# The seam between experts and attention: maxima turned one tile sooner, first scores around k's projection, q and y copied by VectorE

## The chip, the cores and the metric

The kernel runs on one core of one Trainium2 chip. The metric is device time in microseconds of one execution, as the median of several runs. Lower is better.

## The reference, cut to what matters

```python
# x: (8, 512, 128): 8 batches of 512 tokens, 16 heads of 8, 8 experts of width 176, 2 chosen, a shared expert of 352
xn = layernorm(x)
qkv = xn @ w_in.T + b_in                       # q, k, v to 16 heads of 8
scores = (q / sqrt(8)) @ k.T + causal_bias
attn = softmax(scores) @ v                     # then @ w_out.T + b_out, NaN to 0
p = softmax(xn @ gate_w.T)                     # router: 2 largest, normalised, times 2.5 -> combine
y = sum_e combine[:, e] * (silu(xn @ w_gate[e]) * (xn @ w_up[e])) @ w_down[e]
y += (silu(xn @ sw_gate) * (xn @ sw_up)) @ sw_down
out = x + attention + y
```

Everything is float32.

## The kernel before, in words

The five engines each have a program written out by hand, in order, with semaphores between them; nothing reorders it. The work goes batch by batch. For a batch `b` there are two stages, and the program loops over them with the next batch's preparation mixed in:

- **Experts and maxima** (`experts_and_maxima`, the first batch has its own `first_experts_and_maxima`). The 1408 routed and 352 shared hidden columns make `NT` = 14 tiles. For tile `k` TensorE runs `gate_up` (six matmuls, L537 to L539, each product split into high and low float32r parts), ScalarE takes `silu` (L871), POOL weighs it with the router's numbers (L1016, routed tiles), VectorE multiplies by the up half (`hidden`, L1229), ScalarE rounds to the high part (`high_hidden`, L878), POOL takes the low part (`low_hidden`, L1024); VectorE does these two itself for the last tiles (L1237, L1244). Two tiles later TensorE runs `down` (L553 to L555), which adds into `bank_y`. In between, TensorE computes the attention scores a first time, and VectorE takes each row's maximum (L1253). When all are there, VectorE splits the maxima into three bf16 parts (L1274, L1277), TensorE turns them (`transpose_maxima`, L617), ScalarE copies them out (`max_rows`, L900), and a transfer on SP's queue (L433) writes them into `q_op`, where they act as extra rows of q, so that the second computation of the scores has the maximum already taken off.
- **Attention** (`attend`). 20 units of transposed scores (`scores_t`, L646), each into one of two pairs of PSUM banks; ScalarE's exponential of each (L934); POOL's causal mask (L1044); TensorE's product with v (`weigh_v`, L673).

The seam between the two stages also carries the next batch's preparation: TensorE turns its normalised tokens (`transpose_x`, L482), ScalarE copies them (`take_xT`, L845), TensorE projects k (`project_k`, L487), v and router logits (`project_v_and_logits`, L503) and, once v and the logits have been taken out of their bank, q (`project_q`, L496). ScalarE copies k and q out of PSUM with scale and bias (`take_k` L854, `take_q` L849), and also the expert output (`take_y`, L918), which TensorE then turns back (`transpose_y`, L624) so that VectorE adds it to the tokens (`add_tokens`, L1309). VectorE takes the logits' maximum (`router_logits`, L1174, L1176), takes v (`take_v`, L1162), splits k and then q into three bf16 parts (`split_k`, `split_q`, L1145 to L1151), adds the tokens, and computes the router's weights.

What sets the order around the seam: on TensorE each `scores_t` of unit n waits until the exponential of unit n - 2 has emptied its banks, and an instruction that waits holds everything behind it. In `weigh_v` the first product of a batch waits until q has been copied out of its bank:

```python
if g % 2 == 0 and front:
    pe.wait_ge((q_done, k_done)[g // 2], i + 2)
```

`transpose_y` waits for `y_taken`, `project_q` for `v_done` and the logits. On ScalarE the program of `attend` begins with `take_k`, and `take_y`, `exp_router` and `take_q` stand between the first four exponentials.

Of the kernel before, what the change touches and what calls it, by code (L numbers as in the profile page):

```python
# [8 lines left out]
ALU = mybir.AluOpType  # L9
# [43 lines left out]
MAXIMA_AT = NT - 2  # L53
MAXIMA_AT_FIRST = NT - 2
UNITS_FIRST = [3 * int(4 <= k <= 9) for k in range(NT + 2)]
# [60 lines left out]
def block_kernel(nc, x, wqkT, wvT, b_qk, b_v, woT, b_o, gateT, w_gu, w_dn, ident, causal, lower, out):  # L116
    ctx = ExitStack()
    with ctx:
# [358 lines left out]
        def _(pe):  # L477
# [250 lines left out]
            def first_experts_and_maxima():  # L728

                n = 0  # L730
                for k in range(NT + 2):
                    if k == 1:
                        transpose_comb(0)
                    units = UNITS_FIRST[k]
                    if units:
                        pair(0, None, n)
                    if k < NT:
                        gate_up(0, k)
                    if units >= 2:
                        pair(0, None, n + 1)  # L740
                    if k == NT:
                        project_k(1)
                        project_v_and_logits(1, vl)
                        scores_t(0, 0, 0)
                    if k == NT + 1:
                        scores_t(0, 0, 1)
# [6 lines left out]
                    if k == MAXIMA_AT_FIRST:  # L753
                        transpose_x(1)
                    n += units

            def experts_and_maxima(b, i, front):

                n = EARLY
                for k in range(NT + 2):  # L760
# [9 lines left out]
                    if k == NT:  # L770
                        if front:
                            project_k(b + 1)
                            project_v_and_logits(b + 1, vl)
                        scores_t(b, 0, 0)
                    if k == NT + 1:
                        scores_t(b, 0, 1)
# [11 lines left out]
                    if k == MAXIMA_AT and front:  # L788
# [48 lines left out]
        def _(act):  # L837
# [54 lines left out]
            def experts(b, i, front):  # L892
                for k in range(NT):
                    silu(b, k)
                    if k == NT - 1:

                        nc.scalar.activation(table_call[:, :], bqk[:, 1:2], ACT.Exp)
                    if k == NT - 2:
                        act.wait_ge(mT_ready, b + 1)
                        nc.scalar.activation(max_rows[:, :], bank_m[0:HALF, :].bitcast(BF16), ACT.Copy  # L900
                                             ).then_inc(mrows_done, 1)
                        high_hidden(b, k - 1)
                        if front:
                            take_xT(b + 1)
# [11 lines left out]
            def take_y(i):  # L916
                act.wait_ge(down_done, NT * i + NT)
                nc.scalar.activation(yT[:, :], bank_y[:, :], ACT.Copy).then_inc(y_taken, 1)  # L918

            def attend(i, front):  # L920
                if front:
                    take_k(i + 1)
                for g in range(GROUPS):
                    for u in range(UNITS):
                        n = UNITS * g + u
                        act.wait_ge(st_ready, ST_ALL * i + n + 1)
# [9 lines left out]
                        if (g, u) == (0, 1):  # L936
                            take_y(i)
                        if front:
# [134 lines left out]
        def _(dve):  # L1073
# [230 lines left out]

            def add_tokens(b):
# [253 lines left out]
```

## Time and profile before

| | |
|---|---|
| time, median of 3 runs | 576.78 us (576.66 to 577.15) |
| the profiled execution, its own time | 575.52 us |
| its span | 573.8 us |
| busy: PE, DVE, ACT, POOL | 522.2, 452.5, 344.8, 322.3 us |
| granted TensorE clock, mean | 0.994 |

The span is what the profiler saw of the program itself; the rest of the execution's own time lies around it. PE is TensorE, DVE VectorE, ACT ScalarE, POOL GpSimd, SP the queue of most transfers. Busy time is an average over the two stages, which have different limits, so it is read by stage. In a timeline each row is one instruction, or several alike in a row, with its start, its length, and in brackets how long the engine had been idle and what ended that. An instruction on VectorE or ScalarE can start a little before the one ahead of it has ended in the record, so where a chain is added up, the differences between starts are used.

### The profile page before, as it was taken

Reading aid. Unit: us, or ns where it says so; the run is one execution under the profiler, and the core shown is the slowest. Engines: PE = TensorE matmul, PEld = TensorE weight load, DVE = VectorE, ACT = ScalarE, POOL = GpSimd, SP = SyncE. Lnnn points to the kernel's source line nnn. Section 1 sums busy time; section 2 is a strip of 40 time slices with the busy share of each in tenths; the row PEclk is TensorE's granted clock in tenths of the full one; section 3 lists DMA queues with packets and bytes.
Section 4 is the critical chain, followed back from the end, with each engine's and each line's share of the span. In section 5 each row is a group of like instructions: output and inputs, shape, how many; then the busy total and the mean of one; then the engine's idle time right before and its main releaser. Section 6 shows DMA issues by size and latency. Waiting matters only on the chain.

```text
span 573.8 us, 13133 instructions
## 1 busy us (share of the span) xinstructions
PE 522.2 (91%) x4536; PEld 295.5 (51%) x4536; DVE 452.5 (79%) x852; ACT 344.8 (60%) x463; POOL 322.3 (56%) x345
## 2 busy tenths in 40 slices
PE   2679999989999999999999999999999999999985
PEld 1345633656346752576436662466525764366522
DVE  5989798897869968797868968699687978589604
ACT  6422597355963479434983469634794349734693
POOL 2036743775447835479255864478355782558552
PEclk9899999999999999999999999999999999999999
DMA  8984037500475006900268004740069003580001
GB/s 269 267 221 114 12 125 206 132 2 9 146 198 138 2 11 194 261 22 0 104 181 200 0 9 153 220 104 0 22 184 261 18 0 119 164 207 1 10 1 37
DMA packets 45405, 61.99 MB, mean 108 GB/s; under 512 B 4960, under 2 KB 28992, under 8 KB 45376
## 3 DMA queue, kind: packets, MB, share of 16 engines
q1 hardware_dynamic: 42668, 58.37, 36.2%
q10 hardware_dynamic: 2708, 3.24, 1.9%
q8 instruction: 18, 0.29, 0.2%
q14 instruction: 11, 0.09, 0.1%
HBM read 45.21 MB, written 15.34 MB: 106 GB/s over the span
## 4 chain that ended last, share of the span: by engine, by line
PE 60%; DVE 13%; ACT 11%; issue 8%; POOL 5%; DMA 2%; ACTq 1%; POOLq 0%; DVEq 0%
PE banks L673 10%; ACT probs L934 8%; PE banks L537 7%; PE banks L538 6%; PE banks L539 6%; PE banks L573 6%; PE banks L553 6%; PE banks L646 6%; DVE neg_max L1253 5%; PE banks L555 3%; PE banks L554 3%; POOL hid_lo L1024 2%; DVE probs L1229 2%; POOL probs L1044 1%; POOL probs L1016 1%
## 5 line engine op out<-in xcount | busy, mean ns | idle before, releaser
L1253 DVE TENSOR_REDUCE neg_max<-banks 128x2 f32<-128x1024 f32 (+7 forms) x240 | 178.3, 794 | 17.2 <-PE banks L564 16.8
L934 ACT ACTIVATE probs<-banks 128x1024 f32<-128x1024 f32 x160 | 155.4, 1031 | 11.4 <-PE banks L646 9.2
L1044 POOL TENSOR_SCALAR_AFFINE_SELECT probs<-probs 128x512 f32<-128x512 f32 x128 | 90.8, 732 | 124.0 <-ACT probs L934 124.0
L1016 POOL TENSOR_TENSOR probs<-probs,cb 128x512 f32<-128x512 f32 x88 | 113.2, 1286 | 81.4 <-ACT probs L871 80.9
L871 ACT ACTIVATE probs<-banks 128x512 f32<-128x512 f32 (+1 forms) x112 | 67.0, 598 | 134.2 <-PE banks L539 133.9
L1024 POOL TENSOR_TENSOR hid_lo<-probs,hid_hi 128x512 fp32r<-128x512 f32 x85 | 109.6, 1290 | 36.6 <-ACT hid_hi L878 36.3
L1229 DVE TENSOR_TENSOR probs<-probs,banks 128x512 f32<-128x512 f32 (+1 forms) x112 | 76.4, 683 | 35.8 <-POOL probs L1016 27.7
L537 PE MATMUL banks<-x_hi,w_hi 128*128 128x512 f32 (+1 forms) x224 | 95.0, 424 | 4.4 <-DVE probs L1229 4.4
L673 PE MATMUL banks<-probs,v_op 128*32 128x512 f32 (+3 forms) x1024 | 95.2, 444 | 3.7 <-POOL probs L1044 3.5
L538 PE MATMUL banks<-x_lo,w_hi 128*128 128x512 f32 (+1 forms) x224 | 89.0, 398 | 0.0
L539 PE MATMUL banks<-x_hi,w_lo 128*128 128x512 f32 (+1 forms) x224 | 88.8, 396 | 0.0
L878 ACT ACTIVATE hid_hi<-probs 128x512 fp32r<-128x512 f32 (+1 forms) x96 | 60.4, 629 | 43.4 <-DVE probs L1229 43.3
L646 PE MATMUL banks<-q_op,k_op 64*128 64x384 bf16 (+3 forms) x512 | 62.8, 302 | 11.6 <-ACT probs L934 11.3
L573 PE MATMUL banks<-k_op,q_op 64*64 64x448 bf16 (+7 forms) x1024 | 54.2, 293 | 9.8 <-DVE neg_max L1253 7.0
L553 PE MATMUL banks<-hid_hi,wd_hi 128*128 128x512 f32 (+1 forms) x112 | 55.3, 493 | 4.2 <-POOL hid_lo L1024 3.6
L646 PEld LDWEIGHTS banks<-q_op,k_op 64*128 64x128 bf16 x512 | 17.4, 94 | 79.9 <-ACT probs L934 57.4
L537 PEld LDWEIGHTS banks<-x_hi,w_hi 128*128 128x128 f32 (+1 forms) x224 | 42.0, 187 | 20.6 <-DVE probs L1229 5.4
L539 PEld LDWEIGHTS banks<-x_hi,w_lo 128*128 128x128 f32 (+1 forms) x224 | 42.0, 188 | 10.7
L538 PEld LDWEIGHTS banks<-x_lo,w_hi 128*128 128x128 f32 (+1 forms) x224 | 42.1, 188 | 7.8 <-issue 0.2
L573 PEld LDWEIGHTS banks<-k_op,q_op 64*64 64x64 bf16 x1024 | 21.0, 105 | 46.8 <-issue 44.6
L555 PE MATMUL banks<-hid_lo,wd_hi 128*128 128x512 f32 (+1 forms) x112 | 44.7, 399 | 0.0
L554 PE MATMUL banks<-hid_hi,wd_lo 128*128 128x512 f32 (+1 forms) x112 | 44.4, 396 | 0.0
(136 smaller groups left out, 552.3 us busy)
## 6 DMA issues: line engine op xcount, KB each, us to landing
cb<-c_dram SPq DMA_DIRECT2D x31, 256.0 KB, 3.9
q_op<-q_dram SPq DMA_DIRECT2D x15, 512.0 KB, 6.8
k_op<-k_dram SPq DMA_DIRECT2D x15, 512.0 KB, 8.2
cb<-c_dram SPq DMA_DIRECT2D x16, 224.0 KB, 4.3
q_dram<-q_parts SPq DMA_DIRECT2D x8, 384.0 KB, 2.5
k_dram<-k_parts SPq DMA_DIRECT2D x8, 384.0 KB, 2.5
cb<-c_dram SPq DMA_DIRECT2D x16, 192.0 KB, 4.2
cb<-c_dram SPq DMA_DIRECT2D x15, 160.0 KB, 4.3
```

The lines of the kernel that those rows point to most:

```text
L537: pe.matmul(bank, w_hi[:, w, cols], x_hi[:, :], start=True, stop=False)
L538: pe.matmul(bank, w_hi[:, w, cols], x_lo[:, :], start=False, stop=False)
L539: pe.matmul(bank, w_lo[:, w, cols], x_hi[:, :], start=False, stop=True).then_inc(ready, 1)
L553: pe.matmul(bank_y[:, :], wd_hi[0:n, tile, :], hi, start=(k == 0), stop=False)
L573: pe.matmul(bank[rows, a, at:at + n], q_op[own, 2 * g + c, HALF * jq:HALF * (jq + 1)], k_op[own, 2 * g + c, 0:n], start=first, stop=False, ...
L646: mm = pe.matmul(bank[:, at:at + S - kb * P], k_op[r:r + HALF, h // 2, kb * P:(kb + 1) * P], q_op[r:r + HALF, h // 2, kb * P:S], start=Tru ...
L673: mm = pe.matmul(bank[32 * j:32 * j + 32, kb * P:S], v_op[:, kb, g % 2, 4 * (g // 2) + j, :], probs_of(g, j, kb), start=(c == 0 and g % 2 ...
L934: nc.scalar.activation(probs[:, g % 2, 2 * u:2 * u + 2, :], ring[:, at:at + 2, :], ACT.Exp).then_inc(exp_done, 1)
L1016: nc.gpsimd.tensor_tensor(sg[k % 3][:, :], sg[k % 3][:, :], cb[:, tiles_of(b)[k], :], ALU.mult).then_inc(weighted, 1)
L1024: nc.gpsimd.tensor_tensor(hid_lo[0:n, k % 3, :], hid[k % 3][0:n, :], hid_hi[0:n, k % 3, :].bitcast(F32), ALU.subtract).then_inc(hid_lo_don ...
L1044: return nc.gpsimd.affine_select(out=view, in_=view, compare_op=ALU.is_ge, fill=0.0, base=0, pattern=[[0, 4], [1, P]], channel_multiplier=-1)
L1253: return nc.vector.tensor_reduce(out, in_, AX.X, ALU.max, negate=True)
```

## The change

Four things are changed, all in the order of the programs.

1. In all batches but the first, the maxima are turned at tile 11 instead of 12 (`MAXIMA_AT`), on TensorE and, with it, in ScalarE's copy `max_rows`. The turn of the next tokens stays at tile 12 there (`TURN_X_AT`). In the first batch the maxima stay, and the turn of the tokens and its copy move one tile later.
2. On TensorE the first scores go ahead: unit 0 before k's projection, unit 1 behind it, unit 2 already at the last `down`, and the projection of v and logits moves behind unit 2. q's projection moves behind unit 3, and `transpose_y` behind unit 5 (that is, `(g, u) == (1, 0)`).
3. On ScalarE the load of the exponential's table stands at the head of `attend` and `take_k` behind the first exponential. `take_y` and `take_q` are gone from it (the very first q is still copied there).
4. On VectorE `take_q` and `take_y` come between `split_k` and `split_q`.

```diff
-MAXIMA_AT = NT - 2
+MAXIMA_AT = NT - 3
 MAXIMA_AT_FIRST = NT - 2
+TURN_X_AT = NT - 2
...
                     if k == NT:
+                        scores_t(b, 0, 0)
                         if front:
                             project_k(b + 1)
+                        scores_t(b, 0, 1)
+                    if k == NT + 1:
+                        scores_t(b, 0, 2)
+                        if front:
                             project_v_and_logits(b + 1, vl)
-                        scores_t(b, 0, 0)
-                    if k == NT + 1:
-                        scores_t(b, 0, 1)
...
-                        if g < GROUPS and (g, u) not in ((0, 0), (0, 1)):
+                        if g < GROUPS and (g, u) not in ((0, 0), (0, 1), (0, 2)):
                             scores_t(i, g, u)
-                        if front and (g, u) == (0, 2):
+                        if front and (g, u) == (0, 3):
                             project_q(i + 1)
-                        if (g, u) == (0, 3):
+                        if (g, u) == (1, 0):
                             transpose_y(i)
...
             def attend(i, front):
-                if front:
-                    take_k(i + 1)
+                load_exp()
                 for g in range(GROUPS):
                     for u in range(UNITS):
                         n = UNITS * g + u
+                        if front and n == 1:
+                            take_k(i + 1)
                         act.wait_ge(st_ready, ST_ALL * i + n + 1)
...
-                        if (g, u) == (0, 1):
-                            take_y(i)
-                        if front:
-                            if (g, u) == (0, 1):
-                                exp_router(i + 1)
-                            if (g, u) == (0, 2):
-                                take_q(i + 1)
+                        if front and (g, u) == (0, 2):
+                            exp_router(i + 1)
...
+            def take_y(i):
+                dve.wait_ge(down_done, NT * i + NT)
+                nc.vector.tensor_copy(yT[:, :], bank_y[:, :]).then_inc(y_taken, 1)
+
+            def take_q(j):
+                dve.wait_ge(q_ready, j + 1)
+                nc.vector.tensor_scalar(qk_f[:, 0, :], nat[:, 0, :], QSCALE, bq_scaled[:, 0:1], ALU.mult, ALU.add
+                                        ).then_inc(q_done, 1)
...
                     take_v(i + 1, vl)
                     split_k(i + 1)
+                    take_q(i + 1)
+                take_y(i)
+                if front:
                     split_q(i + 1)
                 add_tokens(i)
```

The rows of the changed kernel below carry its own line numbers, one higher on TensorE.

TensorE at the end of a batch's experts, before: k's projection (L487), v and logits (L503), then unit 0 of the scores (L646) and the `down` of tile 12.

```order
L487 MATMUL banks<-xnT,wqk_sb 128x512
L503 MATMUL banks<-wvg_sb,xnT 128x136 x4
L631 ISA
L632 REGISTER_ALU
L646 MATMUL banks<-q_op,k_op 128x512 x2
L553 MATMUL banks<-hid_hi,wd_hi 128x512
L554 MATMUL banks<-hid_hi,wd_lo 128x512
L555 MATMUL banks<-hid_lo,wd_hi 128x512
```

The same place now.

```order
L647 MATMUL banks<-q_op,k_op 128x512 x2
L488 MATMUL banks<-xnT,wqk_sb 128x512
L647 MATMUL banks<-q_op,k_op 128x512 x2
L554 MATMUL banks<-hid_hi,wd_hi 128x512
L555 MATMUL banks<-hid_hi,wd_lo 128x512
L556 MATMUL banks<-hid_lo,wd_hi 128x512
L637 REGISTER_ALU
L647 MATMUL banks<-q_op,k_op 128x384
L647 MATMUL banks<-q_op,k_op 128x128
L647 MATMUL banks<-q_op,k_op 128x384
L647 MATMUL banks<-q_op,k_op 128x128
L504 MATMUL banks<-wvg_sb,xnT 128x136 x4
```

Unit 0 moved from behind two projections to ahead of both, and v and logits moved from ahead of unit 0 to behind units 0, 1 and 2, k's projection and a `down`.

TensorE at the turn of y (L624, out of `o_sb`), before: behind unit 3 and ahead of unit 4.

```order
L496 MATMUL banks<-xnT,wqk_sb 128x512
L646 MATMUL banks<-q_op,k_op 128x384
L646 MATMUL banks<-q_op,k_op 128x128
L646 MATMUL banks<-q_op,k_op 128x384
L646 MATMUL banks<-q_op,k_op 128x128
L624 MATMUL banks<-ident_sb,o_sb 128x128 x4
L646 MATMUL banks<-q_op,k_op 128x256 x4
L646 MATMUL banks<-q_op,k_op 128x512 x2
L673 MATMUL banks<-probs,v_op 32x512 x4
```

The same place now.

```order
L497 MATMUL banks<-xnT,wqk_sb 128x512
L647 MATMUL banks<-q_op,k_op 128x256 x4
L647 MATMUL banks<-q_op,k_op 128x512 x2
L625 MATMUL banks<-ident_sb,o_sb 128x128 x4
L674 MATMUL banks<-probs,v_op 32x512 x4
L647 MATMUL banks<-q_op,k_op 128x512 x2
```

The turn moved two units later; behind it stand the first product with v (L674) and unit 6.

VectorE at the same time, before: the last step of k's split, then the first two of q's.

```order
L1149 CAST k_parts<-qk_rest 128x512 [waits ksplit_step]
L1150 REGISTER_ALU
L1151 TENSOR_TENSOR k_parts<-qk_rest,k_parts 128x512 [waits ksplit_step]
L1145 CAST q_parts<-qk_f 128x512 [waits q_written,q_done]
L1147 TENSOR_TENSOR qk_rest<-qk_f,q_parts 128x512 [waits qsplit_step]
```

The same place now, with the copies of q (L1309) and of y (L1305).

```order
L1147 CAST k_parts<-qk_rest 128x512 [waits ksplit_step]
L1148 REGISTER_ALU
L1149 TENSOR_TENSOR k_parts<-qk_rest,k_parts 128x512 [waits ksplit_step]
L1309 TENSOR_SCALAR qk_f<-banks,bq_scaled 128x512 [waits q_ready]
L1304 ISA
L1305 COPY o_sb<-banks 128x512 [waits down_done]
L1143 CAST q_parts<-qk_f 128x512 [waits q_written,q_done]
```

Both copies stand behind the whole of k's split.

## Rows read from the trace of the kernel before

**Rows 1.** The page: its chain that ended last, shares of the span by engine.

```profile
PE 60%; DVE 13%; ACT 11%; issue 8%; POOL 5%; DMA 2%; ACTq 1%; POOLq 0%; DVEq 0%
```

**Rows 2.** One batch's attention: stretch, length, busy PE, PEld, DVE, ACT, POOL, clock, DMA.

```profile
343.70:364.90 21.20, 19.69 (x183) 6.21 (x183) 17.34 (x38) 20.39 (x24) 10.00 (x14) 1.00 0.48 149
```

**Rows 3.** Timeline of ScalarE at that batch's seam (start, length, instruction).

```profile
342.45 0.69 ACT L854 ACTIVATE qk_f<-banks,bqk 128x512 f32<-128x512 f32 x1
343.70 1.02 ACT L934 ACTIVATE probs<-banks 128x1024 f32<-128x1024 f32 x1 [0.56 <-PE banks L646]
...
345.92 0.59 ACT L918 ACTIVATE o_sb<-banks 128x512 f32<-128x512 f32 x1
...
347.42 0.70 ACT L849 ACTIVATE qk_f<-banks,bq_scaled 128x512 f32<-128x512 f32 x1
347.99 14.71 ACT L934 ACTIVATE probs<-banks 128x1024 f32<-128x1024 f32 x15
...
350.83 1.02 ACT L934 ACTIVATE probs<-banks 128x1024 f32<-128x1024 f32 x1
```

**Rows 4.** Timeline of TensorE at the same seam.

```profile
341.39 1.02 PE L487 MATMUL banks<-xnT,wqk_sb 128*128 128x512 f32 x2
342.25 1.09 PE L503 MATMUL banks<-wvg_sb,xnT 128*128 128x136 f32 x8
...
343.27 0.39 PE L646 MATMUL banks<-q_op,k_op 64*128 64x512 bf16 x2
343.59 0.50 PE L553 MATMUL banks<-hid_hi,wd_hi 128*128 128x512 f32 x1
...
344.49 0.39 PE L646 MATMUL banks<-q_op,k_op 64*128 64x512 bf16 x2
...
347.42 0.65 PE L624 MATMUL banks<-ident_sb,o_sb 128*128 128x128 f32 x4
...
349.40 1.06 PE L673 MATMUL banks<-probs,v_op 128*32 128x512 f32 x8
350.40 0.39 PE L646 MATMUL banks<-q_op,k_op 64*128 64x512 bf16 x2
```

**Rows 5.** Timeline of VectorE at the same seam, and its copy of a full PSUM bank later.

```profile
343.67 0.18 DVE L1174 TENSOR_REDUCE rt_s<-banks 128x4 f32<-128x32 f32 x1
...
344.49 0.69 DVE L1162 TENSOR_TENSOR v_new<-banks,bv_bc 128x512 f32<-128x512 f32 x1 [0.41 <-issue]
345.09 0.42 DVE L1145 CAST k_parts<-qk_f 128x512 bf16<-128x512 f32 x1
...
347.14 0.69 DVE L1151 TENSOR_TENSOR k_parts<-qk_rest,k_parts 128x512 bf16<-128x512 f32 x1
...
360.01 0.68 DVE L1291 COPY o_sb<-banks 128x512 f32<-128x512 f32 x1
```

**Rows 6.** Timelines of the engines at that batch's last expert tiles.

```profile
334.84 0.63 ACT L878 ACTIVATE hid_hi<-probs 128x512 fp32r<-128x512 f32 x1
...
335.23 0.50 PE L553 MATMUL banks<-hid_hi,wd_hi 128*128 128x512 f32 x1 [0.28 <-POOL hid_lo L1024]
...
336.38 1.29 POOL L1024 TENSOR_TENSOR hid_lo<-probs,hid_hi 128x512 fp32r<-128x512 f32 x1
...
338.19 1.02 ACT L900 ACTIVATE max_rows<-banks 64x1024 bf16<-64x1024 bf16 x1 [0.67 <-PE banks L617]
...
339.76 0.69 DVE L1244 TENSOR_TENSOR hid_lo<-probs,hid_hi 128x512 fp32r<-128x512 f32 x1
...
340.69 0.40 PE L553 MATMUL banks<-hid_hi,wd_hi 128*128 128x512 f32 x1
```

**Rows 7.** Timeline of ScalarE in the first batch's attention (units 0 and 6) and the last batch's.

```profile
72.62 1.03 ACT L934 ACTIVATE probs<-banks 128x1024 f32<-128x1024 f32 x1 [0.57 <-PE banks L646]
...
80.07 1.02 ACT L934 ACTIVATE probs<-banks 128x1024 f32<-128x1024 f32 x1
...
545.60 15.61 ACT L934 ACTIVATE probs<-banks 128x1024 f32<-128x1024 f32 x16
```

More of the change, by code:

```diff
@@ L741, in first_experts_and_maxima @@
                     if k == NT:
+                        scores_t(0, 0, 0)
                         project_k(1)
+                        scores_t(0, 0, 1)
+                    if k == NT + 1:
+                        scores_t(0, 0, 2)
                         project_v_and_logits(1, vl)
-                        scores_t(0, 0, 0)
-                    if k == NT + 1:
-                        scores_t(0, 0, 1)
                     if k == MAXIMA_AT_FIRST:
@@ L752, in first_experts_and_maxima @@
                         pair(0, None, n + 2)
-                    if k == MAXIMA_AT_FIRST:
+                    if k == NT - 1:
                         transpose_x(1)
@@ L770, in experts_and_maxima @@
                     if k == NT:
+                        scores_t(b, 0, 0)
                         if front:
                             project_k(b + 1)
+                        scores_t(b, 0, 1)
+                    if k == NT + 1:
+                        scores_t(b, 0, 2)
+                        if front:
                             project_v_and_logits(b + 1, vl)
-                        scores_t(b, 0, 0)
-                    if k == NT + 1:
-                        scores_t(b, 0, 1)
                     if k == MAXIMA_AT:
@@ L787, in experts_and_maxima @@
                         n += 1
-                    if k == MAXIMA_AT and front:
+                    if k == TURN_X_AT and front:
                         transpose_x(b + 1)
@@ L894, in experts @@
                     silu(b, k)
-                    if k == NT - 1:
-                        nc.scalar.activation(table_call[:, :], bqk[:, 1:2], ACT.Exp)
-                    if k == NT - 2:
+                    if k == (MAXIMA_AT_FIRST if i is None else MAXIMA_AT):
                         act.wait_ge(mT_ready, b + 1)
@@ L901, in experts @@
                                              ).then_inc(mrows_done, 1)
+                    if k == NT - 2:
                         high_hidden(b, k - 1)
-                        if front:
-                            take_xT(b + 1)
+                    if front and k == (NT - 1 if i is None else NT - 2):
+                        take_xT(b + 1)
                     if i is None and k == 1:
@@ L914, in experts, with load_exp @@
                         nc.scalar.activation(o_normT[:, :], nat[:, 0, :], ACT.Copy).then_inc(onT_done, 1)
-            def take_y(i):
-                act.wait_ge(down_done, NT * i + NT)
-                nc.scalar.activation(yT[:, :], bank_y[:, :], ACT.Copy).then_inc(y_taken, 1)
+            def load_exp():
+                nc.scalar.activation(table_call[:, :], bqk[:, 1:2], ACT.Exp)
             def attend(i, front):
-                if front:
-                    take_k(i + 1)
+                load_exp()
                 for g in range(GROUPS):
@@ L935, in attend @@
                                              ).then_inc(exp_done, 1)
-                        if (g, u) == (0, 1):
-                            take_y(i)
-                        if front:
-                            if (g, u) == (0, 1):
-                                exp_router(i + 1)
-                            if (g, u) == (0, 2):
-                                take_q(i + 1)
+                        if front and (g, u) == (0, 2):
+                            exp_router(i + 1)
             def weights_in():
```

## The prediction, made before the run

> **What bounds the kernel now.** The chain of waits on the page comes first: TensorE carries 60% of it, with VectorE, ScalarE and POOL taking turns in the rest [rows 1]. A mean like that hides the stages, so the next view is the table of one batch's attention: 21.20 us long, in which ScalarE is busy for 20.39 and TensorE for 19.69 [rows 2]. The reader should see that ScalarE has only 0.81 us to spare there. The timeline of ScalarE then says where: from 347.99 on 15 exponentials take 14.71 us, 0.98 each, with no gap [rows 3]. So attention is paced by the exponentials, and whatever puts off one of them after the first few is not won back before the next batch's experts begin. The spare time lies ahead of 347.99, in the seam, where a copy of y (0.59) and of q (0.70) also stand between exponentials [rows 3]. The change works on that seam. There are seven seams with a next batch behind them and one, the last, without.
>
> What I ask of the change is therefore one number: when does the exponential of unit 6 start? Before, it starts at 350.83 and is held by ScalarE alone [rows 3]; its scores begin at 350.40 [rows 4].
>
> **The change part by part.** I count from S, the start of unit 0's scores on TensorE. Before, S is 343.27 [rows 4], and unit 6's exponential comes 350.83 - 343.27 = 7.56 us later.
>
> *The tail of the experts decides the new S.* Unit 0 now stands right behind the `down` of tile 11, which before began at 340.69 and gave way to k's projection at 341.39 [rows 4, 6]. The maxima's turn itself costs nothing at tile 11: TensorE idled 0.28 us there for POOL anyway, and the turn leaves tile 12 [rows 6]. But the copy `max_rows` holds ScalarE for 1.02 us and follows the turn's start by about the 0.67 us that ScalarE idled for it [rows 6]. With the turn at about 334.9 it runs from 335.5 to 336.5, and the rounding of tile 10, which ran at 334.84, starts behind it at about 336.4 and ends at 337.0. POOL's low part of tile 10, which started at 336.38, then starts near 337.08, 0.70 later [rows 6]. POOL has no gap there, so its weighing of tile 12 is 0.70 later too, VectorE's low part of tile 11 moves from 339.76 to 340.46 and ends at 341.15, and the `down` of tile 11 starts at 341.18 instead of 340.69 [rows 6]. So S is about 341.39 + 0.49 = 341.88. Bounds: 341.2 if nothing on POOL moves, 342.9 if the whole 1.55 us by which the rounding is late passes through. I take 341.88, as the rows give it engine by engine. The maxima's transfer lands earlier than before and doesn't wait.
>
> *TensorE from S to v and logits.* Unit 0 takes 0.32 (343.27 to 343.59), k's projection 0.86 (341.39 to 342.25), unit 1 0.32, the `down` of tile 12 0.90 (343.59 to 344.49), unit 2 0.32 [rows 4]. v and logits start at S + 2.72; before, they started ahead of S. Their row is 1.09 long [rows 4], and with 0.05 for the signal VectorE can take the logits at S + 3.86.
>
> *VectorE from there to y.* Logits to v: 344.49 - 343.67 = 0.82, which holds 0.41 of loop issue; v: 0.60; k's split from 345.09 to the end of its last step at 347.83: 2.74 [rows 5]. Then come the two copies that are new on this engine. The nearest row is VectorE's own copy of a full PSUM bank, 0.68 [rows 5]; two in a row give 0.60 from start to start, as v's row does (0.69 long, next at 0.60), so 0.60 + 0.69. Bounds: 0.42, the row of a cast of the same size out of SBUF [rows 5], and 0.70, ScalarE's copy of q [rows 3]. I take 0.68, the same engine, source and size. Sum: 0.82 + 0.60 + 2.74 + 0.60 + 0.69 = 5.45, so y is out at S + 9.31.
>
> *TensorE waits for it.* Between v and logits and the turn of y it has only a `down`, units 3, 4 and 5, and q's projection, which must wait for v (S + 3.86 + 0.82 + 0.69 = S + 5.37) and then runs about 0.86 like k's. So it stands at the turn near S + 6.9 and **waits about 2.4 us**, with the first product with v and unit 6 queued behind. The turn then takes 0.65, the product 1.00 (349.40 to 350.40) and the exponential starts 0.43 after its scores (343.27 to 343.70) [rows 3, 4]: 9.31 + 0.05 + 0.65 + 1.00 + 0.43 = **S + 11.44**.
>
> *A middle seam.* 341.88 + 11.44 = 353.32, against 350.83: **+2.49 us**. Earlier gains don't survive: unit 0's exponential may start a microsecond sooner, and y and q no longer stand between the first ones, but units 0 to 5 then simply end early and ScalarE waits for unit 6. Behind unit 6 the exponentials run without a gap as before, so the delay stays. VectorE's later work (q's split, tokens, router) moves back by nearly three microseconds, its operands' and the router's transfers with it; as TensorE is 2.5 later as well, I cost that at nothing. That cover is thin only if a transfer was already waited for, and in this attention no row shows one.
>
> The Trainium skill speaks for the copies: its page ScalarE: Activation LUTs, section Rules for kernel authors, says that simple arithmetic belongs on VectorE, which is up to about three times as fast per element in bf16. These copies are float32 out of PSUM, and here VectorE's copy is 0.68 against 0.59 on ScalarE [rows 3, 5]. By that rule each copy would take 0.2, a seam would lose 1.5 instead of 2.5, and the time would be 587; the row decides.
>
> *The first seam* took 80.07 - 72.62 = 7.45 from unit 0's exponential to unit 6's, where the middle one took 350.83 - 343.70 = 7.13 [rows 3, 7], and its VectorE has no loop branch before v, 0.41 [rows 5]. So 2.49 - 0.32 - 0.41 = **+1.8**. *The last seam* has no split ahead of y, so nothing waits; 16 exponentials already ran without a gap there [rows 7], and y's copy of 0.59 leaves ScalarE while the turn moves in front of unit 6. I take 0, between -1.2 and +0.7.
>
> **Sum.** 6 x 2.5 + 1.8 + 0 = **+16.8 us**. Against the profiled execution: 575.52 + 16.8 = 592.3. The median of the runs shown is 1.26 above that execution, 576.78, so I forecast **593.6 us**, about 2.9% slower. What a measurement of this kernel can tell from no change is about 0.2%, 1.2 us.
>
> **The rivals.**
>
> *It does what its parts suggest: faster.* The exponential of unit 0 starts up to 1.25 us sooner, where k's copy stood (342.45 against 343.70), and 0.59 + 0.70 leave the chain [rows 3]; with k's copy moved behind unit 0 (0.69), unit 6 would start about 1.6 us sooner: 7 x 1.6 = 11, 565.6 us. For it: ScalarE is the pace. It decides at the turn of y: y would have to be out about 2.4 us sooner, and k's split alone is 2.74 of the chain ahead of it. It would hold if VectorE met the copies before the split, which its order doesn't show. Chance 0.03.
>
> *The delay is absorbed: no change.* That needs some 2.5 us of waiting on ScalarE behind unit 6; the whole attention has 0.81 [rows 2]. Chance 0.02.
>
> *A smaller loss.* POOL absorbs the late rounding (S = 341.2) and the copies are nearer 0.42 than 0.68: 2.49 - 0.68 - 0.5 = 1.3 a seam, 8 to 9 in all, 586. Against it: POOL's rows stand end to end. Chance 0.12.
>
> *A larger loss.* More of the 1.55 us of late rounding passes, up to 342.9 for S, or VectorE's late router holds TensorE a second time in the same attention: 3.5 a seam, 24 in all, 601. The granted clock was 1.00 throughout that stage [rows 2], with no wait of 2.4 us in it, so what such waits do to the clock isn't shown; a fall would add here. Chance 0.08.
>
> *My forecast*, one wait of 2 to 3 us in each of seven seams: 0.75.
>
> **How the numbers follow.** 593.6 is the forecast. Seams of 1.6 to 3.2 us with the last one's bounds give 587 to 599, which also takes in half of the smaller loss. Slower by over 0.2%: 0.75 + 0.12 + 0.08 = 0.95; within 0.2%: 0.02; faster: 0.03.
>
> **What would show it.** In the changed kernel's timeline TensorE idles 2 to 3 us in front of the turn of y, released by VectorE's copy into `o_sb`, in seven of eight attentions; the exponentials of units 0 to 3 run sooner and a gap of about that length stands ahead of unit 6. POOL's low part of tile 10 starts about 0.7 us later than its place in the order before, released by ScalarE. The last batch shows no such wait. The forecast is wrong if the turn of y waits for under 1 us, if a longer wait stands elsewhere, or if the exponentials behind unit 6 show gaps that take the delay up.

## The result and the profile after

The changed kernel takes **605.91 us** (median of 4 runs, 603.61 to 607.15) against 576.79 (576.66 to 577.15) for the kernel before on the same chip: ratio 1.0499, 95% interval 1.0465 to 1.0533. The forecast was 593.6 with a range of 587 to 599. The direction is right, and the loss is 29.1 us instead of 16.8. The profiled execution has a span of 603.5 us, 29.7 above the span before.

First the page of the changed kernel: its busy times and its chain.

```profile
PE 534.4 (89%) x4536; PEld 294.1 (49%) x4536; DVE 455.9 (76%) x867; ACT 338.1 (56%) x448; POOL 320.9 (53%) x345
PE 58%; DVE 16%; issue 9%; ACT 7%; POOL 6%; DMA 2%; DVEq 0%; POOLq 0%; ACTq 0%
```

ScalarE is busy for 6.7 us less than before (344.8), as the fifteen copies that left it (eight of y, seven of q) suggest, and its share of the chain fell from 11% to 7% [rows 1]. VectorE's rose from 13% to 16%. TensorE has the same 4536 matmuls, but is busy for 12.2 us longer than the 522.2 before. Work that is the same and takes longer is the first sign of a slower clock: the mean granted clock is 0.975 against 0.994.

The list of waits of the changed kernel (total us, times, longest) says who waits for whom.

```profile
ACT probs L937 <- PE banks L647: 40.0, 35, 3.9
PE banks L625 <- DVE o_sb L1305: 16.6, 7, 2.6
```

The second row is the wait that was forecast: TensorE at the turn of y, behind VectorE's copy into `o_sb`, seven times, 2.37 us on the mean. The first row is larger than that wait can explain: the exponentials wait 40.0 us for scores. The same line of the kernel before read 9.2 us:

```profile
ACT probs L934 <- PE banks L646: 9.2, 24, 0.6
```

Now one middle seam. TensorE's timeline after, from unit 0 of the scores to the second product with v:

```profile
358.07 0.39 PE L647 MATMUL banks<-q_op,k_op 64*128 64x512 bf16 x2
358.39 1.12 PE L488 MATMUL banks<-xnT,wqk_sb 128*128 128x512 f32 x2
359.45 0.39 PE L647 MATMUL banks<-q_op,k_op 64*128 64x512 bf16 x2
...
361.00 1.19 PE L504 MATMUL banks<-wvg_sb,xnT 128*128 128x136 f32 x8
...
365.06 0.61 PE L647 MATMUL banks<-q_op,k_op 64*128 64x256 bf16 x6
368.04 0.66 PE L625 MATMUL banks<-ident_sb,o_sb 128*128 128x128 f32 x4 [2.37 <-DVE o_sb L1305]
368.62 1.79 PE L674 MATMUL banks<-probs,v_op 128*32 128x512 f32 x8
370.35 0.61 PE L647 MATMUL banks<-q_op,k_op 64*128 64x512 bf16 x2
370.89 1.50 PE L674 MATMUL banks<-probs,v_op 128*32 128x384 f32 x8
```

Read the last three rows against the same instructions in [rows 4]. The first product with v took 1.06 and now takes 1.79; unit 6 of the scores took 0.39 and now 0.61. The table of stretches of the changed kernel says why (length, busy PE, PEld, DVE, ACT, POOL, then the granted clock, DMA share, GB/s):

```profile
367.00:369.00 2.00, 0.96 (x8) 0.58 (x12) 1.97 (x4) 0.44 (x1) 0.32 (x1) 0.96 0.70 248
369.00:371.00 2.00, 2.00 (x14) 0.22 (x10) 1.90 (x6) 0.00 (x0) 0.00 (x0) 0.50 0.42 145
371.00:373.00 2.00, 2.00 (x20) 0.37 (x21) 1.86 (x5) 1.26 (x2) 0.64 (x1) 0.69 0.98 346
373.00:375.00 2.00, 1.54 (x22) 0.48 (x18) 1.76 (x8) 2.00 (x3) 0.14 (x1) 1.00 0.14 47
```

**Right behind the wait TensorE's clock falls to 0.50, the 1.2 GHz level,** and it is back at 1.00 some three microseconds later. Before, it was 1.00 in the whole stretch [rows 2]. What that does to the exponentials stands in ScalarE's timeline after, which answers to [rows 3]:

```profile
312.19 1.94 ACT L937 ACTIVATE probs<-banks 128x1024 f32<-128x1024 f32 x2 [0.24 <-PE banks L647]
...
358.59 1.01 ACT L937 ACTIVATE probs<-banks 128x1024 f32<-128x1024 f32 x1
...
371.00 1.02 ACT L937 ACTIVATE probs<-banks 128x1024 f32<-128x1024 f32 x1 [3.56 <-PE banks L647]
372.76 10.74 ACT L937 ACTIVATE probs<-banks 128x1024 f32<-128x1024 f32 x11 [0.74 <-PE banks L647]
...
430.16 1.01 ACT L937 ACTIVATE probs<-banks 128x1024 f32<-128x1024 f32 x1
```

The exponential of unit 6 (371.00) waits 3.56 us, the next one 0.74, and the ten behind that run without a gap. From the first exponential of this batch to that of the next the kernel now takes 430.16 - 358.59 = 71.57 us. Before it was 410.41 - 343.70 = 66.71 [rows 3]:

```profile
410.41 1.03 ACT L934 ACTIVATE probs<-banks 128x1024 f32<-128x1024 f32 x1 [0.57 <-PE banks L646]
```

So a middle batch loses 4.86 us where 2.49 was forecast. Split in two: from the first exponential to the end of the last, the attention takes 27.10 instead of 21.18 us, +5.9. From that end to the next batch's first exponential it takes 44.47 instead of 45.53, -1.06: unit 0's exponential does start sooner, as the change means it to.

### The profile page after: what moved, and what is told of

The parts are those of the page before. It is cut to its first block, busy times and chain, and to the rows that moved or that the text cites. A ratio compares the mean times of both kernels' runs of the same rounds, so it can differ in the third digit from the quotient of the medians.

```text
span 603.5 us, 13138 instructions
## 1 busy us (share of the span) xinstructions
PE 534.4 (89%) x4536; PEld 294.1 (49%) x4536; DVE 455.9 (76%) x867; ACT 338.1 (56%) x448; POOL 320.9 (53%) x345
## 4 chain that ended last, share of the span: by engine, by line
PE 58%; DVE 16%; issue 9%; ACT 7%; POOL 6%; DMA 2%; DVEq 0%; POOLq 0%; ACTq 0%
PE banks L674 10%; PE banks L538 7%; PE banks L540 6%; PE banks L574 6%; PE banks L539 6%; PE banks L647 5%; PE banks L554 5%; ACT probs L937 5%; DVE neg_max L1251 5%; POOL hid_lo L1022 3%; PE banks L556 3%; PE banks L555 3%; POOL probs L1014 2%; PE banks L504 2%; DVE probs L1227 1%
## 5 line engine op out<-in xcount | busy, mean ns | idle before, releaser
L1042 POOL TENSOR_SCALAR_AFFINE_SELECT probs<-probs 128x512 f32<-128x512 f32 x128 | 89.1, 717 | 151.2 <-ACT probs L937 151.2
L674 PE MATMUL banks<-probs,v_op 128*32 128x512 f32 (+3 forms) x1024 | 102.6, 475 | 3.7 <-POOL probs L1042 3.5
```

The lines of the kernel that those rows point to most:

```text
L674: mm = pe.matmul(bank[32 * j:32 * j + 32, kb * P:S], v_op[:, kb, g % 2, 4 * (g // 2) + j, :], probs_of(g, j, kb), start=(c == 0 and g % 2 ...
L1042: return nc.gpsimd.affine_select(out=view, in_=view, compare_op=ALU.is_ge, fill=0.0, base=0, pattern=[[0, 4], [1, P]], channel_multiplier=-1)
```

## The experiments

Each ran on the same chip as the kernel before, whose median there was 576.75 to 576.96 us; the ratios are to that median. "Attention" below is the time from the first exponential of a middle batch to the end of its last, "batch" the time from first exponential to first exponential (before: 21.18 and 66.71).

### The clock alone: TensorE kept busy during the wait

Nine spare matmuls, as long together as the wait, stand ahead of the turn of y. Their result is used by nobody. If only the clock makes the extra loss, it goes; the wait's own cost stays.

```diff
+            def keep_busy(n):
+                for _ in range(n):
+                    pe.matmul(bank_m, w_hi[:, 0, 0:P], x_hi[:, :], start=True, stop=True)
...
                         if (g, u) == (1, 0):
+                            if front:
+                                keep_busy(9)
                             transpose_y(i)
```

> The changed kernel with nine spare matmuls on TensorE (their result is read by nobody) ahead of each turn of y that has a next batch, so that the engine works through most of its 2.4 us of waiting for y. Theory (the wait itself costs about 2.5 us a seam, and the clock that fell to 0.50 right behind it costs the rest): the granted clock stays 1.00 behind the turn, the first product with v is back at about 1.06 us, the turn still starts when y is out, and the time is 591 to 596 us, some 12 us below the changed kernel. Rival (the clock falls for another reason of the new order, such as more idle gaps in the whole seam): the product stays near 1.8 us and the time stays at 603 to 608 us.

Measured: **597.77 us** (596.01 to 598.62), ratio to before 1.0348 (1.0308 to 1.0388, against 1.0499 for the changed kernel), so 8.1 us less than the changed kernel, for more work. TensorE's timeline at the same seam:

```profile
355.75 0.39 PE L647 MATMUL banks<-q_op,k_op 64*128 64x512 bf16 x2
...
363.27 2.37 PE L797 MATMUL banks<-x_hi,w_hi 128*128 128x512 f32 x9
365.72 0.66 PE L625 MATMUL banks<-ident_sb,o_sb 128*128 128x128 f32 x4
366.30 1.07 PE L674 MATMUL banks<-probs,v_op 128*32 128x512 f32 x8
```

and the stretch of its table behind the turn:

```profile
366.00:368.00 2.00, 2.00 (x22) 0.54 (x20) 1.90 (x4) 0.27 (x1) 0.00 (x0) 1.00 0.79 275
```

The turn of y comes no sooner (9.97 us behind unit 0 in both kernels), the clock stays at 1.00, and the product is back at 1.07. The attention is 25.49 long instead of 27.10, so the clock costs 1.6 us a seam. The result lies 1.8 above the range expected, which was drawn around the forecast's 593.6: what is left is a middle batch 3.3 us longer than before (426.26 - 356.28 = 69.98), not 2.49. The section on the reasons says where the rest is.

### The order on VectorE: the copies ahead of k's split

If k's split ahead of the copies makes the wait, it goes when the copies stand first.

```diff
                     take_v(i + 1, vl)
-                    split_k(i + 1)
-                    take_q(i + 1)
                 take_y(i)
                 if front:
+                    take_q(i + 1)
+                    split_k(i + 1)
                     split_q(i + 1)
```

> The changed kernel with VectorE's copies of y and of q ahead of k's split instead of behind it; all else is the same. Theory (TensorE waits because k's split, 2.7 us, stands ahead of the copy of y): the wait at the turn of y falls from 2.4 us to under 0.3 us, the clock stays 1.00, unit 6's exponential starts about 1 us later than in the kernel before instead of 5 us, and the time is 580 to 587 us. Rival (VectorE's copies are dear in themselves, or the late v and logits hold everything): 595 us or more.

Measured: **601.32 us** (598.53 to 602.32), ratio 1.0403 (1.036 to 1.0447): a miss by 14 us, on the side of the rival in which the late v and logits hold everything, and the most useful one. The wait at the turn of y is gone; TensorE's timeline shows no idle time there, but a new wait eleven microseconds later:

```profile
367.26 0.66 PE L625 MATMUL banks<-ident_sb,o_sb 128*128 128x128 f32 x4
...
378.68 0.28 PE L511 MATMUL banks<-ident_sb,comb 128*32 128x128 f32 x1 [2.22 <-DVE comb L1208]
```

This is the turn of the router's weights, which VectorE finishes behind k's and q's splits. In the batch shown the clock stays at 1.00. The same wait of 2.22 us stands at 448.17 in the next batch, and there the table shows the clock fall again:

```profile
450.00:452.00 2.00, 2.00 (x14) 0.31 (x10) 1.76 (x3) 1.51 (x2) 0.64 (x1) 0.50 0.81 186
```

The attention is 25.07 us long in the first of the two and 26.47 in the second, and in both the exponential of unit 6 comes 9.0 us behind that of unit 0, 1.9 later than before, where 1 was expected. So the copies cannot simply be moved forward on VectorE. Its whole chain from the logits to the router is late, and what is put behind in it is waited for in its turn.

### Parts alone

The maxima one tile sooner, on the kernel before:

```diff
-MAXIMA_AT = NT - 2
+MAXIMA_AT = NT - 3
+TURN_X_AT = NT - 2
...
-                    if k == NT - 2:
+                    if k == (MAXIMA_AT_FIRST if i is None else MAXIMA_AT):
                         act.wait_ge(mT_ready, b + 1)
```

> The kernel before with the earlier turn of the maxima alone (and ScalarE's copy of them with it); the tokens' turn stays. Theory (that copy puts off ScalarE's rounding of tile 10, which POOL then waits for by 0.7 us): the `down` of tile 11 and all behind it is about 0.5 us later in each of seven batches, 579 to 581 us. Rival one (POOL makes it up): 576 to 577.5 us. Rival two (the maxima's transfer was waited for and its earlier start is a gain): under 575.5 us.

Measured: **580.91 us** (579.70 to 581.94), ratio 1.0065 (1.0047 to 1.0084), as expected. A middle batch takes 67.35 us, +0.64, all of it between the attentions (46.17 against 45.53). The forecast's +0.49 for this part was nearly right; its mechanism shows in POOL's timeline, where the low part of tile 10 waits for ScalarE's rounding behind `max_rows`:

```profile
341.25 1.28 POOL L1026 TENSOR_TENSOR hid_lo<-probs,hid_hi 128x512 fp32r<-128x512 f32 x1 [0.75 <-ACT hid_hi L879]
```

The two copies on VectorE, on the kernel before:

```diff
-                        if (g, u) == (0, 1):
-                            take_y(i)
...
-                            if (g, u) == (0, 2):
-                                take_q(i + 1)
...
                     split_k(i + 1)
+                    take_q(i + 1)
+                take_y(i)
+                if front:
                     split_q(i + 1)
```

> The kernel before with the copies of q and y on VectorE alone, behind k's split as in the change; the scores, the projections and the maxima stay where they were. Theory (any turn of y behind k's split makes TensorE wait, here from 347.4 to about 349.1 in the batch shown, with units 4 to 6 behind it): a wait of about 1.7 us, unit 6's exponential 1.3 to 1.5 us late, 585 to 588 us if the clock stays, up to 596 us if a wait of 1.7 us brings it down too. Rival (ScalarE is the pace and gains the two copies): 566 to 572 us.

Measured: **585.16 us** (583.87 to 586.97), ratio 1.0136 (1.0093 to 1.0179), as expected. The turn of y waits 1.67 us. The clock stays in some batches and falls in others; the last section shows two of them.

The maxima and the early scores, with the copies back on ScalarE (y behind unit 2, q behind unit 3):

```diff
+                        if (g, u) == (0, 2):
+                            take_y(i)
+                        if front and (g, u) == (0, 3):
+                            take_q(i + 1)
...
                     split_k(i + 1)
-                    take_q(i + 1)
-                take_y(i)
```

> The kernel after, but with the copies of y and q back on ScalarE (y behind the exponential of unit 2, q behind that of unit 3): early maxima and first scores around k's projection stay. If the copies on VectorE make the wait at the turn of y, that turn is waited for less than 0.3 us and the 2.37 us go; what stays is that v and the logits come some 2 us later to VectorE, so the router's turn (comb) may wait about 0.4 us, and the exponential of unit 6 starts about 1 us later than in the kernel before: 582 to 588 us, clock mostly 1.00. If the early scores or the early maxima lose the time by themselves, the time stays above 595; if the early scores gain as soon as the copies are gone, it is 577 or less.

Measured: **584.59 us** (583.44 to 585.49), ratio 1.0137 (1.0111 to 1.0163), as expected. TensorE no longer idles at the turn of y, with the same late v and logits:

```profile
355.87 0.66 PE L625 MATMUL banks<-ident_sb,o_sb 128*128 128x128 f32 x4
356.46 1.07 PE L674 MATMUL banks<-probs,v_op 128*32 128x512 f32 x8
```

Two things follow. The early scores, with the late v and logits that come with them, don't pay even without the copies: 584.6 (1.0137) against 580.9 (1.0065) with the maxima alone. And the parts don't add up: the copies alone cost 8.2 us, the rest alone 7.8, together 16.0, but the whole change costs 29.1. The rest makes v and logits late, so that VectorE meets the copies later and TensorE waits 2.37 instead of 1.67; and that longer wait is followed by a slow clock in every middle batch. About 5 of the missing 13 us are the clock: it costs some 8 us in the whole change, by the run with TensorE kept busy, and nearly 3 of that kind are already in the copies alone, two falls of 1.4 us each (last section). Most of the rest goes with the longer wait: at a clock of 1.00 a middle batch loses 0.99 us by the copies alone (67.70 against 66.71), 1.45 by the rest alone (68.16) and 3.27 by the whole change with TensorE kept busy, 0.8 more than the two together, some 5 us in six batches.

### Towards a version that keeps the gain

Five steps, each on the one before; the first starts from the kernel just shown. First, v and logits again early (behind unit 1, ahead of the `down` of tile 12), ScalarE's rounding of tile 10 ahead of `max_rows`, the turn of y one unit later, and the router's weights ahead of the tokens on VectorE:

```diff
                         scores_t(b, 0, 1)
+                        if front:
+                            project_v_and_logits(b + 1, vl)
                     if k == NT + 1:
                         scores_t(b, 0, 2)
...
+                    if k == MAXIMA_AT and i is not None:
+                        high_hidden(b, k - 1)
```

> As the run with the scores alone, and v and logits moved ahead of the scores of unit 2 and the down of tile 12, ScalarE's rounding of tile 10 ahead of its copy of the maxima, the turn of y one unit later, and VectorE's router weights ahead of the tokens. If what is left of the loss is the late start of VectorE's chain and the late rounding, both go, and the exponential of unit 6 starts about 0.7 us sooner than in the kernel before: 571 to 574 us. If the early scores lose for another reason, the time stays at 580 or more.

Then y's copy on VectorE after all, but behind the router's weights, and its turn in the last group, where nothing waits for it:

```diff
                     router_weights(i + 1)
+                take_y(i)
...
-                        if (g, u) == (1, 1):
+                        if (g, u) == (3, 0):
                             transpose_y(i)
```

> As the run with v early, but the copy of y on VectorE as in the change, behind the router weights, with the turn of y in group 3, where nothing waits for it, and tokens and first turn of the attention's output ahead of x's split. If VectorE's copy costs only because it stands in front of work that is waited for, the copy is now free and ScalarE has 0.59 us less: 568 to 572 us. If VectorE has no room for it anywhere, a new wait stands at the turn of the output and the time is 575 or more.

Measured: **576.80 us** (575.07 to 579.28; ratio 1.0003, 0.9991 to 1.0014) and **575.32 us** (574.04 to 578.39; 0.9985, 0.9963 to 1.0006). The loss is gone, but the gain that was expected isn't there: both miss. The first exponential starts 1.7 us sooner than before (43.8 us behind the last end, against 45.53), and the attention is nearly as much longer (22.95 and 22.73 against 21.18). ScalarE's timeline of the second of them shows where:

```profile
346.94 1.02 ACT L939 ACTIVATE probs<-banks 128x1024 f32<-128x1024 f32 x1 [0.95 <-PE banks L647]
...
361.75 2.14 ACT L939 ACTIVATE probs<-banks 128x1024 f32<-128x1024 f32 x2 [0.56 <-PE banks L647]
```

The gaps are now TensorE's: it is busy for 24.79 of the 26.00 us from 335 to 361. That was put to the test by moving the scores of units 2, 3 and 4 one place forward each:

> As the run with y late, where ScalarE idles 0.95 us ahead of the exponential of unit 2 and TensorE is busy 24.79 of 26.00 us of a seam and attention: here the scores of unit 2 stand ahead of v and logits, those of unit 3 ahead of the down of tile 13, those of unit 4 ahead of q's projection. If the order of TensorE in the seam is what still keeps ScalarE waiting, the gap goes and a batch is 0.5 to 0.9 us shorter: 569 to 572 us. If TensorE is by now the pace in itself (its total work, wherever it stands), the gap only moves to unit 4 or behind, and the time is that of the run before, 574 to 577 us.

Measured: **577.99 us** (576.30 to 578.76), ratio 1.0015 (1.0002 to 1.0028). The second reading holds in the trace: the gap of 0.95 goes and comes back, as 0.66 us, behind unit 5. The time is 1 us above the range of that reading, so the new order is, if anything, a little worse. What could still be had is TensorE's own idle time, so y's turn was cut in two halves that fit in the gaps between groups:

```diff
-                        if (g, u) == (3, 0):
-                            transpose_y(i)
+                        if (g, u) == (2, 4):
+                            transpose_y(i, 0)
+                        if (g, u) == (3, 1):
+                            transpose_y(i, 1)
```

> As the run with the scores sooner, with y's turn cut in two halves of 0.33 us, in the group before and in the last one, so that each fits in a gap that TensorE has there (0.46 and 0.24 us). If the turn in one piece is what made the last exponentials wait 0.56 us, 0.2 to 0.4 us a batch go, 1.5 to 3 us below the run with the scores sooner; if TensorE has no gap left there, the time is the same.

Measured: **576.52 us** (575.75 to 578.32), ratio 1.0002 (0.9989 to 1.0016), 1.5 below the run before, at the edge of what was expected. But its middle batches take 66.17 us, 0.54 less than before, and one place gives it all back: the first batch to the second takes 74.14 instead of 70.88. There VectorE also computes statistics, which the late turn of y puts off, and behind them the maxima for which TensorE then waits:

```profile
101.12 0.41 PE L574 MATMUL banks<-k_op,q_op 64*64 64x448 bf16 x6 [3.05 <-DVE neg_max L1261]
...
103.55 1.08 PE L676 MATMUL banks<-probs,v_op 128*32 128x256 f32 x8
```

That product, too, is slow, 1.08 us where the same eight matmuls take 0.64 at 92.89; the clock in the four microseconds from 102 is 0.57. The last version treats the first batch apart: y copied ahead of the router's weights and turned in group 2, the first statistics ahead of the copy of the attention's output.

> As the run with the split turn, whose middle batches take 66.17 us against 66.71 before but whose first seam with the start behind it takes 74.14 against 70.88: there VectorE idles 2.43 us for the turn of y and its statistics then hold up the maxima of the next batch, so that TensorE waits 3.05 us and the clock falls to 0.57. In the first batch alone y is copied ahead of the router weights and turned in group 2, and the first statistics stand ahead of the copy of the attention's output. If that reading is right, the 3 us go and the middle batches stay: 571 to 573.5 us, about 0.7% faster than the kernel before. If the late first batch has another cause, it stays at 575 to 577 us.

Measured: **573.29 us** (572.58 to 574.29), ratio 0.9946 (0.9928 to 0.9965): faster than both kernels, by 0.5% against the one before. The wait of 3.05 is 0.91 now and the clock stays:

```profile
99.19 0.41 PE L574 MATMUL banks<-k_op,q_op 64*64 64x448 bf16 x6 [0.91 <-DVE neg_max L1262]
```

It keeps the change's idea in part (early maxima, early scores, y on VectorE). q's copy went back to ScalarE, and v and logits and the router went forward.

## Why the prediction came out as it did

Step by step, for the middle seam shown above.

**The bound and the place: right.** TensorE idles at the turn of y in seven of eight attentions (2.37 us against "about 2.4"), a late unit 6 isn't won back, and the last batch has no such wait. ScalarE's gap ahead of unit 6 is longer than forecast, 3.56 us where 2 to 3 were said, and one of 0.74 follows it; behind that the exponentials run as before.

**The tail: right to 0.23.** POOL's low part of tile 10 waits 0.74 us for ScalarE (0.70 forecast), as POOL's timeline after shows:

```profile
353.12 1.27 POOL L1022 TENSOR_TENSOR hid_lo<-probs,hid_hi 128x512 fp32r<-128x512 f32 x1 [0.74 <-ACT hid_hi L882]
```

Unit 0's scores were forecast 1.39 us sooner than before (343.27 to 341.88). Counted from the end of the previous exponentials they come 1.16 sooner: before 343.27 - 298.17 = 45.10, after 358.07 - 314.13 = 43.94. (298.17 is where these two end:)

```profile
296.23 1.94 ACT L934 ACTIVATE probs<-banks 128x1024 f32<-128x1024 f32 x2 [0.25 <-PE banks L646]
```

**VectorE's chain to y: 0.61 too short.** The turn of y starts at S + 9.97 instead of S + 9.36. VectorE's timeline after, which answers to [rows 5], gives the parts:

```profile
362.23 0.19 DVE L1172 TENSOR_REDUCE rt_s<-banks 128x4 f32<-128x32 f32 x1 [2.11 <-PE banks L504]
...
363.16 0.69 DVE L1160 TENSOR_TENSOR v_new<-banks,bv_bc 128x512 f32<-128x512 f32 x1 [0.52 <-issue]
363.77 0.42 DVE L1143 CAST k_parts<-qk_f 128x512 bf16<-128x512 f32 x1
...
364.95 0.74 DVE L1147 CAST k_parts<-qk_rest 128x512 bf16<-128x512 f32 x1
365.72 1.00 DVE L1149 TENSOR_TENSOR k_parts<-qk_rest,k_parts 128x512 bf16<-128x512 f32 x1
366.65 0.74 DVE L1309 TENSOR_SCALAR qk_f<-banks,bq_scaled 128x512 f32<-128x512 f32 x1
367.31 0.67 DVE L1305 COPY o_sb<-banks 128x512 f32<-128x512 f32 x1
...
369.08 0.43 DVE L1147 CAST q_parts<-qk_rest 128x512 bf16<-128x512 f32 x1
369.54 0.69 DVE L1149 TENSOR_TENSOR q_parts<-qk_rest,q_parts 128x512 bf16<-128x512 f32 x1
```

The logits reach VectorE at S + 4.16 (3.86 forecast, 0.30 too soon: k's projection takes 1.06 from start to start here, not 0.86, and v and logits come out 0.09 later). From there to v it is 0.93 instead of 0.82, k's split 2.88 instead of 2.74, the two copies 1.33 instead of 1.29, and the signal to TensorE, which was put at 0.05, 0.06. No step is far off; all are off to the same side. Each had been taken from the one row where the same work stood before, and the place has changed. k's projection was followed by another projection there; q's, which was followed by scores, already took 1.06 from start to start, as TensorE's timeline before shows:

```profile
346.03 1.12 PE L496 MATMUL banks<-xnT,wqk_sb 128*128 128x512 f32 x2
347.09 0.40 PE L646 MATMUL banks<-q_op,k_op 64*128 64x384 bf16 x4
```

Ahead of v VectorE's gap is 0.52 instead of 0.41 (rows above and [rows 5]). k's split is longer because its fourth step starts beside a running mask of POOL (1.00), which it didn't before (0.69; last section).

**The path from y to unit 6: the step that failed.** The prediction put 0.65 for the turn, 1.00 for the product and 0.43 from the scores to the exponential, all at the durations of a trace in which the clock never fell. Measured, from start to start: 0.58, 1.73 and 0.65, and then another 0.74 of waiting ahead of the next exponential, because the second product takes 1.50 and not 0.85. That is -0.07 + 0.73 + 0.22 + 0.74 = 1.62 us a seam. The prediction did say under its larger loss that a wait of 2.4 us doesn't occur in that stage before, that its effect on the clock "isn't shown", and that "a fall would add here". But it gave this no price and no condition, left it in a rival at 0.08, whose 601 us the measured time exceeds, and kept it out of the range. The price could have been bounded from its own rows: the products and scores right behind the wait, 1.06 and 0.39 [rows 4], take at most twice as long at the 1.2 GHz level as at 2.4 GHz, so by an estimate up to 1.45 us more a seam from these two. It was this step that took the time out of the range: with TensorE kept busy, and the tail and VectorE's chain as late as they are, 597.77 is still below its 599.

Together: 2.49 + 0.23 + 0.61 + 1.62 = 4.95 for a middle seam, 4.86 measured. Six such seams from batch to batch take 29.3 us more than before, where 15.0 was forecast. The first seam takes 1.2 (1.8 forecast): it waits 2.15 us and keeps its clock. The last attention and the start before the first one give 0.7 back: 29.3 + 1.2 - 0.7 = 29.8, the 29.7 between the two spans.

**The rivals.** "It does what its parts suggest" fell as its own condition said: y would have had to be out 2.4 us sooner. Neither mechanism of the larger loss that was priced is what came: the tail lost less time than it might have (S came 1.16 sooner), and the router's turn isn't waited for in the seam shown. The rule of the Trainium skill (ScalarE: Activation LUTs, Rules for kernel authors) that simple arithmetic is up to about three times as fast per element on VectorE in bf16 would have given 587, by the prediction's estimate. Here VectorE's copy of y takes 0.67 and that of q 0.74, where ScalarE took 0.59 and 0.70 [rows 3]; for these float32 copies out of PSUM the rows decide, and VectorE is the slower one.

## What to carry to other kernels

An in-order engine that takes over work from a busy one is judged by what stands ahead of that work in its queue and by who waits for it, not by its share of busy time: the same copy of y made TensorE wait 2.37 us with its turn in group 1, and none behind the router's weights with its turn in group 3. Where a change adds a wait of microseconds on TensorE, price the matmuls right behind it at the 1.2 GHz level as well, and put that case into the range. And when the engine that sets the pace is relieved, ask at once which engine has the least idle time next: here TensorE was already busy for 24.79 of 26.00 us (y on VectorE, turned late), and where 1.29 us of copies stood, the best of these orders gains 0.54 us a middle batch.

## What the runs showed of the hardware that was not expected

**The same wait can cost the clock or not.** In the kernel with the copies alone, two batches have the same wait at the turn of y. TensorE's timeline:

```profile
286.94 0.66 PE L624 MATMUL banks<-ident_sb,o_sb 128*128 128x128 f32 x4 [1.67 <-DVE o_sb L1302]
...
288.07 1.07 PE L673 MATMUL banks<-probs,v_op 128*32 128x512 f32 x8
...
354.65 0.66 PE L624 MATMUL banks<-ident_sb,o_sb 128*128 128x128 f32 x4 [1.68 <-DVE o_sb L1302]
...
355.78 1.93 PE L673 MATMUL banks<-probs,v_op 128*32 128x512 f32 x8
```

The granted clock is 1.00 behind the first and 0.50 behind the second, and the second attention is 1.4 us longer (23.61 against 22.16). The first batch of the changed kernel waits longer and keeps its clock, too (1.00 from 80 to 82); its timeline:

```profile
79.67 0.66 PE L625 MATMUL banks<-ident_sb,o_sb 128*128 128x128 f32 x4 [2.15 <-DVE o_sb L1305]
80.26 1.06 PE L674 MATMUL banks<-probs,v_op 128*32 128x512 f32 x8
```

The kernel with the copies first has the same wait of 2.22 us in six middle batches; the clock falls at four of them and stays at two (378.68 and 518.57). So for a wait of this size the fall is not a matter of its length alone. Where it falls, it doesn't keep step with the waits: in the changed kernel the six falls begin 0.34, 0.48, 0.66, 0.79, 0.92 and 1.42 us behind the start of the turn (at 153.79, 225.47, 297.15, 368.83, 440.51 and 512.19), evenly 71.68 us apart, while the turns are 71.2 to 71.6 apart. The Trainium skill (TensorE: Matmul & The Clock Gate, in the part on what is actually happening) says that the hardware looks at TensorE's activity in a window that runs freely, whatever the kernel does; that would explain it, and these rows agree with it, but no run here shifted a wait in time on purpose to show it.

**VectorE is slower when it starts beside a running mask of POOL.** The third and fourth steps of k's split take 0.74 and 1.00 us in the seam after, where the same steps of q's split take 0.43 and 0.69 a little later (VectorE's timeline above). POOL's timeline has two masks just then, 1.64 together, where one alone takes 0.63:

```profile
364.54 1.64 POOL L1042 TENSOR_SCALAR_AFFINE_SELECT probs<-probs 128x512 f32<-128x512 f32 x2 [2.58 <-ACT probs L937]
```

The Trainium skill (SBUF — State Buffer, Who interferes with whom) says that VectorE shares a pair of SBUF ports with POOL and meets it there in operations with two SBUF inputs and in copies and casts of a two-port mode. The fourth step has two SBUF inputs, and the trace agrees (1.00 against 0.69); in which mode the cast runs, no run here shows. No mask was moved away to try it, but the masks fall differently in each batch, and the traces sort cleanly. Of the sixteen fourth steps of the changed kernel the seven that start while a mask runs take 1.00 and the nine others 0.69; in the kernel before it is nine and seven with the same lengths, k's at 347.14 among the short ones [rows 5]. What counts is which starts first: the second step at 364.22 begins ahead of the mask at 364.54 and takes its usual 0.69.
